# Expert stage of a two-layer kernel: loads, rounding and slot comparison per pair of sequences

## The chip, the core and the metric

The kernel runs on one core of a Trainium2 chip. The metric is device time in microseconds (us); lower is better. The core has TensorE (PE; its weight loads are listed as PEld), VectorE (DVE), ScalarE (ACT), GpSimd (POOL) and SyncE (SP, which here only issues DMAs). Sixteen DMA engines move data between the core's on-chip memory and HBM.

## The reference

128 sequences of 128 tokens with 256 channels pass two layers, each added to its input. The first is windowed cross attention. The second, the stage that is changed here, is a mixture of 16 experts with top-2 routing:

```
xn2  = layernorm(x1)                       # x1: output of the attention layer
p    = softmax(xn2 @ w_router)             # 16 experts
for the 2 best experts e of each token (slots of e filled in token order, 16 slots a sequence; later ones dropped):
    y += p_e * ( silu(s @ w_gate[e]) * (s @ w_fc[e]) ) @ w_proj[e]     # s: the token's row of xn2
out  = x1 + tanh(g_ffn) * y
```

## The kernel before

**Stages.** One program runs three parts one after another: attention (to about 1210 us of the span), routing (softmax, top 2, slot numbers; to about 1264 us), and the expert stage (the rest, about 490 us). Attention leaves `x1_d` (the residual) and `xn2_d` (the normalised rows) in HBM, both laid out as token, sequence, channel. A partition's 256 channels of one sequence are 1 KB there, and those of two neighbouring sequences are 2 KB in one piece.

**Units.** The expert stage works through 128 units, written as a software pipeline over steps u. Each operation has a lag: it serves unit n = u - lag in step u. For loading, picking and dispatching, n is a sequence; eight sequences form a group. For gate, hidden and output, n is a group and a pair of experts, so that eight units cover a group's 16 experts. For fetching and collecting, n is again a sequence. The work of step u, by lag:

- LOAD (-13): SP loads one sequence of `xn2_d` (128 KB) into a ring of three.
- PICK (-11): ACT rounds it to `x_hi` (fp32r); POOL subtracts for the rest, `x_lo`; DVE compares slot numbers with a table for the 0/1 matrix `pick`. Rings of two.
- DISPATCH (-9): PE multiplies `x_hi` and `x_lo` with `pick` into the PSUM bank `DS` (4 matmuls); ACT copies `s_hi`, DVE subtracts for `s_lo`.
- GATE (0): PE forms gate and up projections in `GU` (12 matmuls); ACT takes `th = tanh(gate/2)`; DVE forms `th = (th + 1) * gate` and `hid = th * up`. This is twice silu(gate) * up, and a factor 0.5 in `weight` (line 984) takes the 2 out.
- HIDDEN (2): PE transposes `hid` into `HT`; ACT copies `h_hi`, DVE subtracts for `h_lo`.
- OUTPUT (3): PE forms the down projection `EO` (6 matmuls); ACT copies it to `eo` and issues the store to `eo_d` (256 KB).
- FETCH (12): SP loads one sequence of the residual from `x1_d` into a ring of three; POOL issues two indirect DMAs that gather the token's two expert rows (`first`, `second`) from `eo_d`.
- COLLECT (14): DVE forms `first * weight + residual`, then adds `second * weight`; SP stores the result to `out`.

**Order.** Each engine runs its own list in program order and waits on semaphores. Within a step, PE does OUTPUT, HIDDEN, GATE, DISPATCH. SP does the store of COLLECT, then LOAD, then FETCH. POOL does the two gathers, then `x_lo`. ACT does `eo`, `h_hi`, the store of `eo`, `x_hi`, `th`, `s_hi`. DVE does `h_lo`, `pick`, first half of COLLECT, the two GATE products, second half of COLLECT, `s_lo`.

**Buffers.** `x_in_sb`, `xr` and `y_sb` of this stage are parts of the routing table `scaled`, under whose name their instructions appear in the profile. So `scaled<-xn_d` is LOAD, `scaled<-x_d` the residual's FETCH, `out<-scaled` the store, `scaled<-first,weight,scaled` (L1229) and `scaled<-second,weight,scaled` (L1244) the two halves of COLLECT. `pick<-logits` reads the slot numbers, kept in the old `logits` tensor as fp32.

Of the kernel before, what the change touches and what calls it, by code (L numbers as in the profile page):

```python
# [25 lines left out]
P = 128  # L26
# [833 lines left out]
def routing_block(nc, ctx, T, D):  # L860
# [82 lines left out]
    def _(dve):  # L943
# [40 lines left out]
        then(dve.tensor_scalar(weight[:], prob[:], gates[:, 3:4], 0.5, ALU.mult, ALU.mult))  # L984
# [23 lines left out]
class Unit:  # L1008
# [35 lines left out]
def expert_block(nc, ctx, T, D):  # L1044


    LOAD, PICK, DISPATCH, GATE, HIDDEN, OUTPUT, FETCH, COLLECT = -13, -11, -9, 0, 2, 3, 12, 14
# [8 lines left out]
    def pb(name):  # L1056
# [3 lines left out]
    tiles = T["scaled"][:].rearrange("p b e -> p (b e)").rearrange("p (n c) -> p n c", c=DIM)  # L1060
    x_in_sb, xr, y_sb = tiles[:, 0:3], tiles[:, 3:6], tiles[:, 6:8]
    x_hi = sb("x_hi", [P, 2, DIM], F32R)
    x_lo = sb("x_lo", [P, 2, DIM], F32R)
    pick = sb("pick", [P, 2, SLOTS], F32R)
    s_hi = sb("s_hi", [P, 2, KC, EXPERTS, GROUP, CAP], F32R)
    s_lo = sb("s_lo", [P, 2, KC, EXPERTS, GROUP, CAP], F32R)
    th = sb("th", [P, 2, 2, HID])
    hid = sb("hid", [P, 2, 2, HID])
# [11 lines left out]
    names = ("x_hi_done x_lo_done pick_done ds_done s_hi_done s_lo_done gu_done th_done "  # L1080
             "gated_done hid_done ht_done h_hi_done h_lo_done eo_done eo_copied y_part_done out_done").split()
    M = {n: sem(n) for n in names}
    x_in = [sem(f"xn2_in{r}") for r in range(3)]
# [3 lines left out]
    y_out = [sem("y_out0"), sem("y_out1")]  # L1087
# [28 lines left out]

    def tokens(buf, n):

        return buf[:, n.side, :, :, n.j].rearrange("p k e s -> p (k e) s")

    @block.sync
    def _(sp):
        def step(unit, on):
            n = unit(COLLECT)
            if on(COLLECT):
                sp.wait_ge(M["out_done"], n.n + 1)
                sp.dma_start(D["out"][bass.ds(n.n, 1)].rearrange("b t c -> t b c"),
                             y_sb[:, n.slot(2):n.slot(2) + 1]).then_inc(y_out[n.slot(2)], 16)
# [40 lines left out]
    def _(act):  # L1169
        def step(unit, on):  # L1170
            n = unit(OUTPUT)
            if on(OUTPUT):
                act.wait_ge(M["eo_done"], n.n + 1)
                wait_for(act, eo_out[n.turn(3)], (n - 3).landed(3))
                act.activation(flat(eo[:, n.turn(3)]), EO[n.slot(2)][:], ACT.Copy).then_inc(M["eo_copied"], 1)
# [7 lines left out]
            if on(OUTPUT):  # L1183
                act.wait_ge(M["eo_copied"], n.n + 1)
                act.dma_start(D["eo_d"][n.group][:, n.j * 2:n.j * 2 + 2], eo[:, n.turn(3)]) \
                    .then_inc(eo_out[n.turn(3)], 16)
            n = unit(PICK)
            if on(PICK):
                act.wait_ge(x_in[n.turn(3)], n.landed(3))
                wait_for(act, M["ds_done"], n.n - 1)  # L1190
                act.activation(x_hi[:, n.slot(2)], x_in_sb[:, n.turn(3)], ACT.Copy).then_inc(M["x_hi_done"], 1)  # L1191
            n = unit(GATE)
            if on(GATE):
                act.wait_ge(M["gu_done"], n.n + 1)
# [13 lines left out]
    def _(dve):  # L1208
        def step(unit, on):
            n = unit(HIDDEN)  # L1210
            if on(HIDDEN):
# [3 lines left out]
                                  flat(h_hi[:, n.slot(2)]).bitcast(F32), ALU.subtract).then_inc(M["h_lo_done"], 1)  # L1215
            n = unit(PICK)
            if on(PICK):
                wait_for(dve, M["ds_done"], n.n - 1)
                dve.tensor_tensor(pick[:, n.slot(2)].rearrange("p (e s) -> p e s", s=CAP),
                                  place[:, bass.ds(n.n, 1)].rearrange("p o (e s) -> p (o e) s", s=1)  # L1220
                                  .broadcast_to([P, EXPERTS, CAP]),
                                  iota[:].rearrange("p (e s) -> p e s", s=CAP), ALU.is_equal) \
                    .then_inc(M["pick_done"], 1)
            n = unit(COLLECT)
            if on(COLLECT):
                dve.wait_ge(rows_in[n.turn(3)], n.landed(3, 32))
                dve.wait_ge(x1_in[n.turn(3)], n.landed(3))
                wait_for(dve, y_out[n.slot(2)], (n - 2).landed(2))
                dve.scalar_tensor_tensor(out=y_sb[:, n.slot(2)], in0=first[:, n.turn(3)],  # L1229
                                         scalar=weight[:, 0, bass.ds(n.n, 1)], in1=xr[:, n.turn(3)],  # L1230
                                         op0=ALU.mult, op1=ALU.add).then_inc(M["y_part_done"], 1)
            n = unit(GATE)
            if on(GATE):
                gu = GU[n.slot(2)][:].rearrange("p (e f n) -> p e f n", e=2, f=2)
                dve.wait_ge(M["th_done"], n.n + 1)
                dve.scalar_tensor_tensor(out=th[:, n.slot(2)], in0=th[:, n.slot(2)], scalar=1.0, in1=gu[:, :, 0],  # L1236
                                         op0=ALU.add, op1=ALU.mult).then_inc(M["gated_done"], 1)
                dve.wait_ge(M["gated_done"], n.n + 1)
                wait_for(dve, M["ht_done"], n.n - 1)
                dve.tensor_tensor(hid[:, n.slot(2)], th[:, n.slot(2)], gu[:, :, 1], ALU.mult).then_inc(M["hid_done"], 1)  # L1240
            n = unit(COLLECT)
            if on(COLLECT):
                dve.wait_ge(M["y_part_done"], n.n + 1)
                dve.scalar_tensor_tensor(out=y_sb[:, n.slot(2)], in0=second[:, n.turn(3)],  # L1244
                                         scalar=weight[:, 1, bass.ds(n.n, 1)], in1=y_sb[:, n.slot(2)],
                                         op0=ALU.mult, op1=ALU.add).then_inc(M["out_done"], 1)
# [136 lines left out]
```

## Time and profile before

| | |
|---|---|
| median of 3 timed runs | 1762.0 us (1760.66 to 1764.96) |
| profiled execution, its own time | 1754.3 us |
| its span | 1752.5 us |
| busy PE / DVE / ACT / POOL, whole span | 85% / 80% / 65% / 62% |
| busy PE / DVE / ACT / POOL, 1320 to 1500 us | 88% / 92% / 56% / 82% |
| DMA share 0 to 1146 us; 1320 to 1500 us | 0.23; 0.84 |

The second busy line is worked out from a windows view of the middle of the expert stage. An average over the whole span says little about it, since attention fills two thirds of the span. Matmul records overlap: one of 128x256 is listed with 0.28 us, but the next starts 0.12 us later. A DVE record also runs on a little after the next has begun, so the distance between two starts is what an instruction costs its engine. "issue" as the end of a wait means that the profile shows no releaser.

### The profile page before, as it was taken

How to read it: one execution, taken by the hardware profiler on the slowest of the kernel's cores; microseconds unless marked ns; L12 is line 12 of the kernel's file. 1: busy time of each engine (PE TensorE's matmuls, PEld its weight loads, DVE VectorE, ACT ScalarE, POOL GpSimd, SP SyncE). 2: the span in 40 equal slices, each digit the busy share in tenths (PEclk: the TensorE clock that was granted, in tenths of full speed). 3: DMA queues.
4: the chain of work that ended last, by engine and by line, in shares of the span. 5: the costliest groups of instructions: out<-in, count | busy, mean ns of one | idle time of the engine just before them, and what ended most of it. 6: DMA issues, size and time to landing. Idle time of an engine off the chain costs nothing. (4 is left out here: it accounts for less than half of the span.)

```text
span 1752.5 us, 50746 instructions
## 1 busy us (share of the span) xinstructions
PE 1481.3 (85%) x16844; PEld 1195.2 (68%) x16844; DVE 1408.6 (80%) x2993; ACT 1146.4 (65%) x2321; POOL 1086.1 (62%) x1490
## 2 busy tenths in 40 slices
PE   3899999999999999999999999982199888888881
PEld 3676667777776676777676677761088888888881
DVE  3788888888888888878888888867878999999984
ACT  3777777777777777777777777764065555555550
POOL 3555656565655656565565656534638887888876
PEclk9999999999999999999999999995589999999995
DMA  3122121212222121212212121430037888888887
GB/s 94 50 76 75 61 89 60 90 60 84 65 67 82 60 90 60 90 60 78 71 62 88 60 90 60 137 119 30 15 106 245 260 261 258 261 273 263 264 261 223
DMA packets 156096, 210.21 MB, mean 120 GB/s; under 512 B 18688, under 2 KB 104832, under 8 KB 156032
## 3 DMA queue, kind: packets, MB, share of 16 engines
q1 hardware_dynamic: 125312, 142.36, 25.9%
q0 software_dynamic: 12288, 33.57, 6.7%
q10 hardware_dynamic: 18432, 33.56, 5.3%
q8 instruction: 24, 0.39, 0.1%
q14 instruction: 40, 0.33, 0.1%
HBM read 125.54 MB, written 83.89 MB: 119 GB/s over the span
## 5 line engine op out<-in xcount | busy, mean ns | idle before, releaser
L506 DVE TRANSPOSE_TENSOR_REDUCE part_max<-ST 128x16 f32<-128x512 f32 x512 | 321.3, 685 | 136.6 <-PE ST L685 136.6
L360 ACT ACTIVATE probs_t<-ST 128x512 f32<-128x512 f32 x512 | 264.4, 604 | 27.6 <-PE ST L700 27.4
L712 PE MATMUL PO<-probs_t,v_aug 128*32 128x128 f32 x4096 | 193.6, 284 | 67.9 <-ACT probs_t L360 55.4
L299 POOL TENSOR_TENSOR k_rot<-k_cos,k_sin 128x256 f32<-128x256 f32 x64 | 47.1, 736 | 268.5 <-DVE k_sin L544 268.5
L712 PEld LDWEIGHTS PO<-probs_t,v_aug 128*32 128x32 f32 x4096 | 88.9, 109 | 161.1 <-ACT probs_t L360 154.0
L1191 ACT ACTIVATE x_hi<-scaled 128x256 fp32r<-128x256 f32 x128 | 53.5, 418 | 214.8 <-DMA scaled<-xn_d 168.5
L401 ACT ACTIVATE at_hi<-F 128x512 fp32r<-128x512 f32 x64 | 38.2, 597 | 187.8 <-PE F L730 187.8
L1260 PE MATMUL GU<-we_hi,s_hi 128*128 128x256 f32 x512 | 155.4, 304 | 0.2 <-DVE s_lo L1250 0.2
L1154 POOL DMA_INDIRECT second<-eo_d,collect_row x128 | 123.0, 961 | 42.2 <-issue 28.6
L1163 POOL TENSOR_TENSOR x_lo<-scaled,x_hi 128x256 fp32r<-128x256 f32 x128 | 118.4, 925 | 49.3 <-ACT x_hi L1191 47.3
L1154 POOL DMA_INDIRECT first<-eo_d,collect_row x128 | 124.4, 972 | 37.3 <-issue 20.6
L1261 PE MATMUL GU<-we_hi,s_lo 128*128 128x256 f32 x512 | 144.9, 283 | 0.0
L1262 PE MATMUL GU<-we_lo,s_hi 128*128 128x256 f32 x512 | 144.8, 283 | 0.0
L316 POOL TENSOR_TENSOR q_rest<-q_rot,q_head 128x512 f32<-128x512 f32 x64 | 82.2, 1284 | 78.7 <-ACT q_head L413 78.7
L1260 PE MATMUL EO<-we_hi,h_hi 128*128 128x256 f32 x256 | 81.6, 319 | 50.3 <-issue 43.5
L730 PE MATMUL F<-ident_sb,xn 128*128 128x128 f32 x512 | 86.2, 292 | 31.1 <-ACT xn L437 19.7
L366 ACT ACTIVATE out_t<-PO 128x512 f32<-128x512 f32 x128 | 76.7, 599 | 53.2 <-PE PO L712 53.2
L1229 DVE SCALAR_TENSOR_TENSOR scaled<-first,weight,scaled 128x256 f32<-128x256 f32 x128 | 65.5, 512 | 49.6 <-issue 18.1
L1261 PEld LDWEIGHTS GU<-we_hi,s_lo 128*128 128x128 f32 x512 | 98.3, 192 | 0.0
L1260 PEld LDWEIGHTS GU<-we_hi,s_hi 128*128 128x128 f32 x512 | 97.6, 191 | 0.4 <-issue 0.4
L1262 PEld LDWEIGHTS GU<-we_lo,s_hi 128*128 128x128 f32 x512 | 97.8, 191 | 0.0
L1260 PEld LDWEIGHTS EO<-we_hi,h_hi 128*128 128x128 f32 x256 | 48.3, 188 | 70.0 <-issue 68.1
(158 smaller groups left out, 5610.7 us busy)
## 6 DMA issues: line engine op xcount, KB each, us to landing
eo_d<-eo ACTq DMA_DIRECT2D x128, 256.0 KB
x_in_sb<-x SPq DMA_DIRECT2D x64, 256.0 KB, 2.8
c_in_sb<-ctx_t SPq DMA_DIRECT2D x64, 256.0 KB, 2.9
xr_sb<-x SPq DMA_DIRECT2D x64, 256.0 KB, 4.0
x_d<-x SPq DMA_DIRECT2D x64, 256.0 KB, 4.0
xn_d<-xn SPq DMA_DIRECT2D x64, 256.0 KB, 4.2
scaled<-xn_d SPq DMA_DIRECT2D x128, 128.0 KB, 4.0
scaled<-x_d SPq DMA_DIRECT2D x128, 128.0 KB
```

Of the source, the lines that this page charges most:

```text
L316: pool.tensor_tensor(q_rest[:].rearrange("p k t -> p (k t)"), q_rot[:].rearrange("p k t -> p (k t)"), q_head[:].rearrange("p k t -> p (k t ...
L360: act.activation(probs_t[:, b, i].rearrange("p j q -> p (j q)"), ST[i][:], ACT.Exp) \
L366: act.activation(out_t[:, b].rearrange("p i q -> p (i q)"), PO[:], ACT.Copy).then_inc(M["ot_copied"], 1)
L506: dve.tensor_reduce(part_max[:, i, 0], ST[i][:].rearrange("p (c l) -> p c l", l=32), AX_X, ALU.max, apply_transpose=True).then_inc(M["part ...
L712: last = pe.matmul(PO[32 * j:32 * j + 32, i * SEQ:(i + 1) * SEQ], v_aug[:, n.par, b, head], probs_t[:, b, i, j], start=True, stop=True)
L730: last = pe.transpose(F[:, (2 * k + b) * SEQ:(2 * k + b + 1) * SEQ], src[:, b, k * P:(k + 1) * P], ident[:])
L1154: pool.indirect_dma_start(out=dst[:, n.turn(3)], out_offset=None, in_=D["eo_d"][n.group].rearrange("r e c -> (r e) c"), in_offset=bass.Ind ...
L1163: pool.tensor_tensor(x_lo[:, n.slot(2)], x_in_sb[:, n.turn(3)], x_hi[:, n.slot(2)].bitcast(F32), ALU.subtract).then_inc(M["x_lo_done"], 1)
L1229: dve.scalar_tensor_tensor(out=y_sb[:, n.slot(2)], in0=first[:, n.turn(3)], scalar=weight[:, 0, bass.ds(n.n, 1)], in1=xr[:, n.turn(3)], op ...
L1260: pe.matmul(out, lh, rh, start=first, stop=False)
L1261: pe.matmul(out, ll, rh, start=False, stop=False)
L1262: return pe.matmul(out, lh, rl, start=False, stop=last)
```

## The change

The units, the matmuls and the bytes moved stay as they are. The parts that change:

- SP loads two sequences of `xn2_d` (LOAD, now lag -14) and two of `x1_d` (FETCH, now 13) with one DMA of 256 KB each, in every other step and by turns. SP's order becomes FETCH, LOAD, store.
- The ring of rows holds four sequences, that of residuals six. COLLECT (now 15) works in place in the residual's ring, so that FETCH waits for the stores of the pair six sequences earlier.
- `x_hi` is one ACT instruction per pair (HEAD, -11) on 512 columns. `x_lo` moves from POOL to DVE, one instruction per pair (REST, -10). `pick` is one instruction per pair on DVE, and reads slot numbers kept in bf16. Their rings hold four.
- ACT computes silu directly, so DVE has one GATE product instead of two, and the factor 0.5 is gone.
- ACT does `h_hi` ahead of `eo`. On DVE, `s_lo` stands between the two halves of COLLECT.
- Buffers get fixed places over the routing tables.

```diff
-    LOAD, PICK, DISPATCH, GATE, HIDDEN, OUTPUT, FETCH, COLLECT = -13, -11, -9, 0, 2, 3, 12, 14
+    LOAD, PICK, HEAD, REST, DISPATCH, GATE, HIDDEN, OUTPUT, FETCH, COLLECT = -14, -11, -11, -10, -9, 0, 2, 3, 13, 15
...
+    def two(a, n, ring):
+        return a[:, n.n % ring:n.n % ring + 2]
+    def pair_landed(n, ring):
+        return (n.n // (2 * ring) + 1) * 16
...
     @block.sync
+            n = unit(FETCH)
+            if on(FETCH) and n.n % 2 == 0:
+                if n.n >= 6:
+                    for k in range(2):
+                        sp.wait_ge(y_out[(n.n + k) % 6], n.n // 6 * 16)
+                sp.dma_start(two(xr, n, 6), D["x1_d"][:, bass.ds(n.n, 2)]).then_inc(x1_in[n.n // 2 % 3], 16)
+            n = unit(LOAD)
+            if on(LOAD) and n.n % 2 == 0:
+                wait_for(sp, M["x_hi_done"], n.n // 2 - 1)
+                wait_for(sp, M["x_lo_done"], n.n // 2 - 1)
+                sp.dma_start(two(x_in_sb, n, 4), D["xn2_d"][:, bass.ds(n.n, 2)]).then_inc(x_in[n.n // 2 % 2], 16)
...
-            n = unit(LOAD)
-            if on(LOAD):
-                wait_for(sp, M["x_hi_done"], n.n - 2)
-                wait_for(sp, M["x_lo_done"], n.n - 2)
-                sp.dma_start(x_in_sb[:, n.turn(3):n.turn(3) + 1], D["xn2_d"][:, bass.ds(n.n, 1)]) \
-                    .then_inc(x_in[n.turn(3)], 16)
-            n = unit(FETCH)
-            if on(FETCH):
-                wait_for(sp, M["y_part_done"], n.n - 2)
-                sp.dma_start(xr[:, n.turn(3):n.turn(3) + 1], D["x1_d"][:, bass.ds(n.n, 1)]) \
-                    .then_inc(x1_in[n.turn(3)], 16)
...
     @block.gpsimd
-            n = unit(PICK)
-            if on(PICK):
-                pool.wait_ge(M["x_hi_done"], n.n + 1)
-                wait_for(pool, M["ds_done"], n.n - 1)
-                pool.tensor_tensor(x_lo[:, n.slot(2)], x_in_sb[:, n.turn(3)], x_hi[:, n.slot(2)].bitcast(F32),
-                                   ALU.subtract).then_inc(M["x_lo_done"], 1)
...
     @block.scalar
+            n = unit(HEAD)
+            if on(HEAD) and n.n % 2 == 0:
+                act.wait_ge(x_in[n.n // 2 % 2], pair_landed(n, 2))
+                wait_for(act, M["ds_done"], n.n - 2)
+                act.activation(flat(two(x_hi, n, 4)), flat(two(x_in_sb, n, 4)), ACT.Copy).then_inc(M["x_hi_done"], 1)
...
-                               ACT.Tanh, scale=0.5).then_inc(M["th_done"], 1)
+                               ACT.Silu).then_inc(M["gate_done"], 1)
...
     @block.vector
+            n = unit(REST)
+            if on(REST) and n.n % 2 == 0:
+                dve.wait_ge(M["x_hi_done"], n.n // 2 + 1)
+                wait_for(dve, M["ds_done"], n.n - 2)
+                dve.tensor_tensor(flat(two(x_lo, n, 4)), flat(two(x_in_sb, n, 4)), flat(two(x_hi, n, 4)).bitcast(F32),
+                                  ALU.subtract).then_inc(M["x_lo_done"], 1)
             n = unit(PICK)
+            if on(PICK) and n.n % 2 == 0:
+                wait_for(dve, M["ds_done"], n.n - 2)
+                dve.tensor_tensor(two(pick, n, 4).rearrange("p b (e s) -> p b e s", s=CAP),
...
+                dve.tensor_tensor(gate[:, n.slot(2)], gate[:, n.slot(2)], gu[:, :, 1], ALU.mult).then_inc(M["hid_done"], 1)
...
-                dve.scalar_tensor_tensor(out=th[:, n.slot(2)], in0=th[:, n.slot(2)], scalar=1.0, in1=gu[:, :, 0],
-                                         op0=ALU.add, op1=ALU.mult).then_inc(M["gated_done"], 1)
...
     @block.tensor
-                pe.wait_ge(M["pick_done"], n.n + 1)
-                pe.wait_ge(M["x_hi_done"], n.n + 1)
-                pe.wait_ge(M["x_lo_done"], n.n + 1)
+                for done in ("pick_done", "x_hi_done", "x_lo_done"):
+                    pe.wait_ge(M[done], n.pair + 1)
...
-        T["place"] = T["logits"]
+        T["place"] = sb("place", [P, SEQS, EXPERTS], BF16)
```

DVE in the middle of the stage, one step before (`hid<-th,GU` is the second GATE product):

```order
L1214 TENSOR_TENSOR h_lo<-HT,h_hi 128x256
L1219 TENSOR_TENSOR pick<-logits,iota_sb 128x256
L1229 SCALAR_TENSOR_TENSOR scaled<-first,weight,scaled 128x256
L1236 SCALAR_TENSOR_TENSOR th<-th,GU 128x256
L1240 TENSOR_TENSOR hid<-th,GU 128x256
L1244 SCALAR_TENSOR_TENSOR scaled<-second,weight,scaled 128x256
L1250 TENSOR_TENSOR s_lo<-DS,s_hi 128x32x16
```

The same place now, two steps (`xr` is the residual's ring, `raw` the ring of rows):

```order
L1216 TENSOR_TENSOR h_lo<-HT,h_hi 128x256
L1222 TENSOR_TENSOR x_lo<-raw,x_hi 128x512
L1237 TENSOR_TENSOR gate<-gate,GU 128x256
L1242 SCALAR_TENSOR_TENSOR xr<-first,weight,xr 128x256
L1248 TENSOR_TENSOR s_lo<-DS,s_hi 128x32x16
L1253 SCALAR_TENSOR_TENSOR xr<-second,weight,xr 128x256
L1216 TENSOR_TENSOR h_lo<-HT,h_hi 128x256
L1227 TENSOR_TENSOR pick<-place,iota_sb 128x512
L1237 TENSOR_TENSOR gate<-gate,GU 128x256
L1242 SCALAR_TENSOR_TENSOR xr<-first,weight,xr 128x256
L1248 TENSOR_TENSOR s_lo<-DS,s_hi 128x32x16
L1253 SCALAR_TENSOR_TENSOR xr<-second,weight,xr 128x256
```

Seven instructions a step become six. The second row of a step is by turns the rest or the comparison of a whole pair.

SP in the middle of the stage, two steps before:

```order
L1127 DMA out<-scaled 128x256
L1133 DMA scaled<-xn_d 128x256
L1138 DMA scaled<-x_d 128x256
L1127 DMA out<-scaled 128x256
L1133 DMA scaled<-xn_d 128x256
L1138 DMA scaled<-x_d 128x256
```

And two steps now:

```order
L1142 DMA raw<-xn_d 128x512
L1146 DMA out<-xr 128x256
L1137 DMA xr<-x_d 128x512
L1146 DMA out<-xr 128x256
```

Six DMAs in two steps become four, and each load stands ahead of its step's store.

## Rows read from the trace of the kernel before

**Rows 1.** Windows: length, busy PE PEld DVE ACT POOL, clock, DMA share, GB/s

```profile
1320.00:1500.00 180.00, 157.68 (x1235) 149.04 (x1233) 166.07 (x357) 101.33 (x257) 147.32 (x154) 1.00 0.84 259
```

**Rows 2.** Who waited for whom, 1320 to 1640 us: total us, times, longest

```profile
PE EO L1260 <- issue: 32.4, 78, 1.2
...
DVE scaled L1229 <- DMA second<-eo_d,collect_row: 0.6, 1, 0.6
```

**Rows 3.** Chain that ended last, at 1361 us: start, us, what

```profile
1361.36 0.34 SPq L1127
...
1361.80 0.46 SPq L1133
...
1362.31 3.70 DMA scaled<-x_d
```

**Rows 4.** Timeline of POOL, 1503 to 1507 us: start, us, instruction

```profile
1503.50 0.96 POOL L1154 DMA_INDIRECT first<-eo_d,collect_row  x1 [0.18 <-issue]
1504.77 0.96 POOL L1154 DMA_INDIRECT second<-eo_d,collect_row  x1 [0.30 <-DMA eo_d<-eo]
1505.75 1.01 POOL L1163 TENSOR_TENSOR x_lo<-scaled,x_hi 128x256 fp32r<-128x256 f32 x1
1506.95 0.97 POOL L1154 DMA_INDIRECT first<-eo_d,collect_row  x1 [0.19 <-issue]
```

**Rows 5.** Timeline of DVE, one step in the middle

```profile
1503.57 0.41 DVE L1219 TENSOR_TENSOR pick<-logits,iota_sb 128x256 fp32r<-128x256 f32 x1
1504.42 0.48 DVE L1229 SCALAR_TENSOR_TENSOR scaled<-first,weight,scaled 128x256 f32<-128x256 f32 x1 [0.44 <-issue]
1504.90 0.42 DVE L1236 SCALAR_TENSOR_TENSOR th<-th,GU 128x256 f32<-128x256 f32 x1
1505.35 0.42 DVE L1240 TENSOR_TENSOR hid<-th,GU 128x256 f32<-128x256 f32 x1
1505.69 0.48 DVE L1244 SCALAR_TENSOR_TENSOR scaled<-second,weight,scaled 128x256 f32<-128x256 f32 x1
1506.09 0.68 DVE L1250 TENSOR_TENSOR s_lo<-DS,s_hi 128x512 fp32r<-128x512 f32 x1
1506.69 0.41 DVE L1214 TENSOR_TENSOR h_lo<-HT,h_hi 128x256 fp32r<-128x256 f32 x1
```

**Rows 6.** Windows, a stretch before the first collect

```profile
1300.00:1310.00 10.00, 10.00 (x85) 9.90 (x84) 7.58 (x18) 6.12 (x17) 2.21 (x3) 1.00 0.45 150
```

**Rows 7.** Timeline of DVE: tanh products of units 4, 12, 14, 127

```profile
1295.86 0.42 DVE L1236 SCALAR_TENSOR_TENSOR th<-th,GU 128x256 f32<-128x256 f32 x1 [0.36 <-ACT th L1196]
...
1319.11 0.42 DVE L1236 SCALAR_TENSOR_TENSOR th<-th,GU 128x256 f32<-128x256 f32 x1 [0.35 <-ACT th L1196]
...
1324.91 0.42 DVE L1236 SCALAR_TENSOR_TENSOR th<-th,GU 128x256 f32<-128x256 f32 x1
...
1714.31 0.42 DVE L1236 SCALAR_TENSOR_TENSOR th<-th,GU 128x256 f32<-128x256 f32 x1
```

**Rows 8.** Groups by form, 1320 to 1640 us: busy us, mean ns, idle

```profile
L1244 DVE SCALAR_TENSOR_TENSOR scaled<-second,weight,scaled 128x256 f32<-128x256 f32 x91 | 68.6, 753 | 0.0
...
L1191 ACT ACTIVATE x_hi<-scaled 128x256 fp32r<-128x256 f32 x92 | 38.4, 418 | 133.1 <-DMA scaled<-xn_d 109.3 <-PE DS L1305 23.8
```

**Rows 9.** The subtraction x_lo over the whole span: ns min/median/max

```profile
L1163 POOL TENSOR_TENSOR x_lo<-scaled,x_hi x128: 722/997/1024, 1266.6 to 1682.8; 128x256 fp32r<-128x256 f32 x128
```

**Rows 10.** DMA queues, 1320 to 1640 us: packets, MB, share of 16

```profile
q1 hardware_dynamic: 39074, 35.58, 37.8%
q0 software_dynamic: 8800, 24.02, 25.9%
q10 hardware_dynamic: 13248, 24.12, 20.8%
```

**Rows 11.** Last gather on POOL, and the DVE instruction that waits for it

```profile
1746.11 0.95 POOL L1154 DMA_INDIRECT second<-eo_d,collect_row  x1 [0.31 <-issue]
...
1749.30 0.48 DVE L1229 SCALAR_TENSOR_TENSOR scaled<-first,weight,scaled 128x256 f32<-128x256 f32 x1 [1.43 <-DMA second<-eo_d,collect_row]
```

More of the change, by code:

```diff
@@ L1021, in group, with pair @@
     @property
+    def pair(self):
+        return self.i * (LOOP // 2) + self.c // 2
+    @property
     def group(self):
@@ L1057, in pb @@
         return ctx.enter_context(nc.psum_tensor(name, [P, 512], F32))
[L1060 to L1064, printed above, removed]
+    x_in_sb, xr, x_hi, x_lo = (T[k][:] for k in ("raw", "xr", "x_hi", "x_lo"))
+    pick = sb("pick", [P, 4, SLOTS], F32R)
     s_hi = sb("s_hi", [P, 2, KC, EXPERTS, GROUP, CAP], F32R)
     s_lo = sb("s_lo", [P, 2, KC, EXPERTS, GROUP, CAP], F32R)
-    th = sb("th", [P, 2, 2, HID])
-    hid = sb("hid", [P, 2, 2, HID])
+    gate = sb("gate", [P, 2, 2, HID])
     h_hi = sb("h_hi", [P, 2, 2, P], F32R)
@@ L1086, in expert_block @@
     eo_out = [sem(f"eo_out{r}") for r in range(3)]
-    y_out = [sem("y_out0"), sem("y_out1")]
+    y_out = [sem(f"y_out{r}") for r in range(6)]
     DS = [pb("DS0"), pb("DS1")]
@@ L1170, in step @@
         def step(unit, on):
[L1171 to L1175, printed above, removed]
             n = unit(HIDDEN)
@@ L1183, in step @@
             if on(OUTPUT):
+                act.wait_ge(M["eo_done"], n.n + 1)
+                wait_for(act, eo_out[n.turn(3)], (n - 3).landed(3))
+                act.activation(flat(eo[:, n.turn(3)]), EO[n.slot(2)][:], ACT.Copy).then_inc(M["eo_copied"], 1)
+            n = unit(OUTPUT)
+            if on(OUTPUT):
                 act.wait_ge(M["eo_copied"], n.n + 1)
@@ L1226, in step @@
                 dve.wait_ge(rows_in[n.turn(3)], n.landed(3, 32))
[L1227 to L1230, printed above, removed]
+                dve.wait_ge(x1_in[n.n // 2 % 3], pair_landed(n, 3))
+                dve.scalar_tensor_tensor(out=xr[:, n.turn(6)], in0=first[:, n.turn(3)],
+                                         scalar=weight[:, 0, bass.ds(n.n, 1)], in1=xr[:, n.turn(6)],
                                          op0=ALU.mult, op1=ALU.add).then_inc(M["y_part_done"], 1)
[L1232 to L1235, printed above, removed]
-                dve.scalar_tensor_tensor(out=th[:, n.slot(2)], in0=th[:, n.slot(2)], scalar=1.0, in1=gu[:, :, 0],
-                                         op0=ALU.add, op1=ALU.mult).then_inc(M["gated_done"], 1)
[L1238 to L1246, printed above, removed]
             n = unit(DISPATCH)
@@ L1251, in step @@
                                   tokens(s_hi, n).bitcast(F32), ALU.subtract).then_inc(M["s_lo_done"], 1)
+            n = unit(COLLECT)
+            if on(COLLECT):
+                dve.wait_ge(M["y_part_done"], n.n + 1)
+                dve.scalar_tensor_tensor(out=xr[:, n.turn(6)], in0=second[:, n.turn(3)],
+                                         scalar=weight[:, 1, bass.ds(n.n, 1)], in1=xr[:, n.turn(6)],
+                                         op0=ALU.mult, op1=ALU.add).then_inc(M["out_done"], 1)
         run_flat(dve, step)
@@ L1280, in step @@
                 for e in range(2):
-                    last = pe.transpose(HT[n.slot(2)][:, e * P:(e + 1) * P], hid[:, n.slot(2), e], ident[:])
+                    last = pe.transpose(HT[n.slot(2)][:, e * P:(e + 1) * P], gate[:, n.slot(2), e], ident[:])
                 last.then_inc(M["ht_done"], 1)
```

57 lines of the change are left out of this document (31 added, 26 removed).

## The prediction

> **What bounds the kernel now.** The change touches the expert stage alone, so I read its stretch first, in the windows view [rows 1]. In 180 us of its middle the clock is at 1.00 (2.4 GHz), PE is busy 157.68 us (88%), DVE 166.07 us (92%), POOL 147.32 us (82%), and the DMA engines 0.84. Nothing is at 100%, so the bound is a loop of waits. The length of a step comes from the DVE timeline: unit 14's tanh product starts at 1324.91 and unit 127's at 1714.31 [rows 7], 389.4 us for 113 steps, or 3.446 us each.
>
> The waits say that PE stands before `EO` 78 times in the stretch [rows 2]. `EO` needs `h_lo`, so PE waits for DVE, and DVE waits for something in turn: in the step shown it idles 0.44 us before the first half of COLLECT (L1229) [rows 5]. The chain shows for what [rows 3]. SP issues the store at 1361.36, `xn_d` at 1361.80, then `x_d`, whose data lands 3.70 us after 1362.31, at 1366.01. From the store's issue to the landing is 4.65 us. From L1229's start (1504.42) to the end of L1244 (1505.69 + 0.48) is 1.75 us [rows 5], and a few tenths go to semaphores. The loop is some 6.8 us, and a residual fetched in step u is used in step u+2: 3.4 us a step, as measured.
>
> There is a second bound of the same size. POOL's step [rows 4] is gather 1.27, gather 0.98, `x_lo` 1.20 from start to start, 3.45 us, with gaps of only 0.18 and 0.30 us. Removing one bound alone would gain next to nothing. Here both go.
>
> PE's own pace is in the windows before the first collect: PE 10.00 us of 10.00 [rows 6]. Tanh products of units 4 and 12 start at 1295.86 and 1319.11 [rows 7]: 23.25 / 8 = 2.906 us a step. That is the floor, since the matmuls stay the same.
>
> **The change, part by part (per step).**
>
> *Residual loads.* Fetched one step earlier against COLLECT, ahead of the step's load and store, two at a time. From the end of `out` of n-3, which SP's previous store waits for, to the first half of n there are now three steps less the time from that half's start to the next end of `out`. That time is 0.40 to 0.48 (first half) + 0.60 (`s_lo`) + 0.48 = 1.5 us [rows 5]. SP needs 0.34 + 0.46 us to issue [rows 3] and the data its landing. For 256 KB under load the trace has no row; bounds are 3.70 us (as 128 KB now) and 7.40 us (twice that). The step that this loop needs is (0.8 + 3.7 + 1.5) / 3 = 2.0 us to (0.8 + 7.4 + 1.5) / 3 = 3.23 us. I take it as below the floor, because bytes per step stay equal and 3.70 us contains the queueing behind the `xn_d` load. The stores that free the ring of six are issued over two steps before the fetch, so that wait is covered.
>
> *Row loads.* ACT's idle time before `x_hi`, 109.3 us for `xn_d` [rows 8], is in nobody's way as long as ACT is 56% busy [rows 1]. The new load has three steps less the time that SP waits for `x_lo` of the same step, some 7 us. Price 0. If it came late, ACT would stand with `gate` and `s_hi` queued behind HEAD, and DVE and PE after it.
>
> *POOL.* `x_lo` goes: two gathers are left, 2 x 1.27 = 2.54 us [rows 4]. Below the floor. The gather's loop (two issues 2.5 us, landing 1747.06 to 1749.30 = 2.2 us [rows 11], 1.5 us to the end of `out`) is 6.2 us for three steps, 2.1 us a step. DVE waited for a gather only 0.6 us in the whole stretch, with two steps of distance [rows 2].
>
> *DVE.* I add distances between starts [rows 5]. Before: pick and the like 0.34, first half 0.48, `th` 0.45, `hid` 0.34, second half 0.40, `s_lo` 0.60, `h_lo` 0.34 (same form as `hid`) = 2.95, plus idle, plus what L1244 loses. It has 0.48 us here and 753 ns in the mean [rows 8], so 0.27 more. Now: `h_lo` 0.34, one pair instruction 0.60 (as `s_lo`, also 512 columns; at most twice a `pick`, 0.82), product 0.34, first half 0.40 to 0.48, `s_lo` 0.60, second half 0.40 = 2.7 us; with the upper pair price 2.98. Value 2.72.
>
> L1244 is slow, and POOL's `x_lo` has 722 ns at least but 997 in the median [rows 9]: the two slow each other. The Trainium skill ("SBUF — State Buffer", the section with the single rule on port contention) says that a DVE instruction with two SBUF inputs contends with a GpSimd instruction that reads SBUF, and that the later one is blocked. By that rule the 0.27 us go with `x_lo`, since what stays on POOL are gathers, and DVE needs 2.72 us; if gathers block as well, it needs 2.99 us and sits just above PE. I take the first.
>
> The sum without the page goes by bounds: L1244 between 0.48 and 0.753 us, taken at 0.48, its value in the step shown, where it starts 0.06 us ahead of `x_lo` (1505.69 against 1505.75 [rows 4]). So DVE is at 2.7 us, or at 3.0 us at worst.
>
> *Latencies inside a step.* PE needs `h_lo` a step after the transposes, and DVE's gate product follows PE's gate matmuls with silu between. With DVE at 2.7 of 2.9 us these fit, but with 0.2 us of slack, and single waits will show. I add 0.03 us a step.
>
> *ACT.* One `x_hi` per pair instead of two of 418 ns [rows 8] can only save; silu in place of tanh keeps shape and count. Price 0.
>
> *DMA.* Shares of the three queues [rows 10] sum to 0.845: 0.845 x 3.446 = 2.91 us of all 16 engines per step. Queue 1 moves three transfers of 128 KB a step: 0.378 x 3.446 x 16 / 3 = 6.95 engine-us each. Queue 10 moves one of 256 KB with rows of 2 KB: 0.208 x 3.446 x 16 = 11.5. The two loads' bytes now travel in 2 KB pieces as well: 13.9 becomes 11.5, so 2.91 falls to 2.76 us. Below the floor, but at a share of 0.94.
>
> *Ends.* Ahead of unit 14 nothing of the above binds. The first load is twice as big (up to one landing more, +3.7 us), while the nine dispatches ahead of unit 0 trade POOL's 0.72 us [rows 9] for half of a 0.60 on DVE (-0.4 us each): value 0, bounds -4 and +3.7. At the end COLLECT lies one unit further back, and the tail is paced by POOL's gathers: one pair more, +2.5 us.
>
> **Sum.** 2.906 + 0.03 = 2.94 us a step. 113 x (3.446 - 2.94) = 57.2 us less, 2.5 us more: 54.7 us. The profiled execution has 1754.3 us and would have 1699.6. The timed runs' median, 1762.0, lies 7.7 us above it, and I keep that: 1707 us.
>
> **Rivals.**
>
> *A: DVE or the DMA engines bind between 3.0 and 3.25 us.* For it: the 0.94 share, the landing's upper bound (3.23 us), DVE's upper sum (3.0 us). Against it: DMA work per step falls, and all loops gained a step of distance. At 3.10 us it is 113 x 0.346 = 39 - 2.5 = 36.6 us less: 1725 us. The Trainium skill ("DMA: Bandwidth & Descriptors", table of the Bandwidth section) gives 341 GB/s for transfers of 1 MB and 138 for 64 KB; a step of 2.94 us asks 917,504 B / 2.94 us = 312 GB/s of transfers of 128 and 256 KB. No run here shows that rate over a long stretch; the 259 GB/s at share 0.84 [rows 1] would reach 308 at full share, and 2 KB pieces raise it.
>
> *B: only one of the two bounds went.* If the residual's or the rows' load still limits at 3.3 to 3.44 us, the gain is under 14 us: about 1752. For it: `x_lo` of the same step is waited for by SP, ahead of the store. Against it: that wait ends early in DVE's step.
>
> *C, slower: the paired loads land too late.* Place: SP's one ring, where 256 KB stand in front of each store and each fetch. It decides once a landing takes over 3 x 3.446 - 1.5 - 0.8 = 8.0 us. At 9 us the step is (9 + 2.3) / 3 = 3.77 us, 37 us + 2.5 more: about 1801. For it speaks only the high share; 3.70 us now against it.
>
> **Chances.** Forecast (2.90 to 3.0 us a step, 1700 to 1714) 0.70; A 0.21; B 0.04, a part of it within 0.3% (about 5 us, what a measurement can tell from no change); C 0.04; the rest lies below 1700. The range 1697 to 1733 leaves out B, C and A's upper end. Faster 0.94, within 0.3% 0.02, slower 0.04.
>
> **What would show it.** Steps of 2.9 to 3.0 us between gate products. PE near 10 of 10 us in windows of the middle, and hardly a wait before `EO`. POOL idle about 0.4 us a step before `first`, waiting for the second half of COLLECT. The second half of COLLECT at 0.48 us. The chain through PE lines and no longer through `x_d`. A DMA share of 0.9 or more. I would be wrong with idle time of DVE before the first half of COLLECT for `xr`, with ACT waiting for `raw` and DVE behind it, or with DVE at 98% and PE waiting.

## The result, and the profile after

| | median of the timed runs | runs |
|---|---|---|
| before | 1762.0 us (1758.8 to 1767.1) | 20 |
| after | 1768.2 us (1763.9 to 1771.3) | 20 |

The ratio is 1.0031, with an interval of 1.0021 to 1.0041: slightly slower. Forecast were 1707 us and a range of 1697 to 1733. The profiled execution has 1766.2 us and a span of 1764.4 us, against 1754.3 and 1752.5 before.

The windows view of the changed kernel, the same stretch as [rows 1] (length, busy PE PEld DVE ACT POOL, clock, DMA share, GB/s):

```profile
1320.00:1500.00 180.00, 153.94 (x1224) 148.71 (x1222) 140.33 (x304) 103.75 (x232) 98.49 (x98) 0.98 0.80 256
```

The work left DVE and POOL as forecast (166 to 140 us, 147 to 98 us busy), and yet PE is busy less than before. The granted clock explains little: 0.98 in place of 1.00 costs at most 2% of the stretch, 3.6 us (an estimate), while at the forecast 2.94 us a step it would hold 61 steps and holds 51. The step is in the starts of the gate product, for the same units 14 and 127 as in [rows 7], again a timeline of DVE (start, us, instruction, idle before it and what ended that):

```profile
1325.45 0.42 DVE L1237 TENSOR_TENSOR gate<-gate,GU 128x256 f32<-128x256 f32 x1
...
1724.68 0.42 DVE L1237 TENSOR_TENSOR gate<-gate,GU 128x256 f32<-128x256 f32 x1 [3.99 <-ACT gate L1198]
```

That is 399.2 us for 113 steps, 3.533 us each instead of 3.446, or 9.8 us more; the ends add 2.1 to make the 11.9 us between the spans. Few steps have that length. Some 30 take 2.66 us, and 48 of the 113 over 3.3, up to 5.9. Who waited for whom, 1320 to 1640 us (total us, times, longest), answers to [rows 2]:

```profile
POOL first L1162 <- DVE xr L1253: 78.9, 42, 8.8
...
PE EO L1264 <- ACT h_hi L1177: 29.2, 23, 1.9
ACT s_hi L1204 <- remote: 24.3, 20, 1.7
ACT h_hi L1177 <- remote: 23.2, 24, 1.7
...
ACT gate L1198 <- remote: 13.2, 6, 2.6
```

No load stands in it: neither ACT waits for `raw` nor DVE for `xr`. New is "remote", which the view of before does not contain. All three instructions of ACT wait for PE and for nothing outside this core. The view writes "remote" where the semaphore's update is on record, just before the waiting instruction starts, but over 1.5 us after the end of the last instruction that makes such an update; where the update has no record at all, it writes "issue". One such place, from the timeline:

```profile
1508.44 0.28 PE L1309 MATMUL DS<-pick,x_lo 128*128 128x256 f32 x1
...
1509.32 0.38 PE L1285 MATMUL HT<-ident,gate 128*128 128x128 f32 x2
...
1510.39 0.60 ACT L1204 ACTIVATE s_hi<-DS 128x512 fp32r<-128x512 f32 x1 [1.70 <-remote]
...
1511.90 0.38 ACT L1177 ACTIVATE h_hi<-HT 128x256 fp32r<-128x256 f32 x1 [0.91 <-remote]
...
1512.84 0.36 PE L1264 MATMUL EO<-we_hi,h_hi 128*128 128x256 f32 x1 [1.27 <-ACT h_hi L1177]
```

The last dispatch matmul ends at 1508.72; its semaphore update is recorded at 1510.37, and `s_hi` starts at 1510.39. The transposes start at 1509.32 and end at 1509.69; their update is recorded at 1511.88, 2.2 us later, and `h_hi` starts at 1511.90. ACT was free 0.91 us before that. So ACT reacts at once, and it is the update that comes late. (The ends of matmuls are modelled; in every trace of chips 7 and 13 the update lies within 0.02 us of them.)

From 1320 to 1640 us the trace holds 266 updates made by PE, of which 115 are recorded over 0.8 us after the matmul's end (the transposes' mostly 2.2, the dispatch's 1.6); of the 550 by ACT and DVE not one is even 0.15 us late. The late ones come in PE's order: here dispatch, output, transposes, gate and dispatch again are recorded 1.6, 1.7, 2.2, 0.9 and 0.5 us after their ends. That is what a backlog looks like that fills and drains.

The chain that ended last says the same (start, us, what); its share of "another core or an unknown queue" is 26.6% from 1480 to 1520 us:

```profile
1508.33 2.04 another core or an unknown queue
1510.41 1.46 another core or an unknown queue
1511.90 0.39 ACT h_hi L1177
1512.29 0.55 issue
1512.84 0.36 PE EO L1264
```

So the gain is taken back by PE's updates reaching ACT 1.6 to 2.2 us after the work is done, in about a third of the steps. Whether the paired loads do it was what the experiments had to find. The third and fourth group of them show that they do not, and that it goes with the chip that the kernel runs on, or with what surrounds it there. What delays the updates stays open.

### The profile page after: what moved, and what is told of

The parts are those of the page before. It is cut to its first block and busy times, and to the rows that moved or that the text cites. A ratio compares the mean times of both kernels' runs of the same rounds, so it can differ in the third digit from the quotient of the medians.

```text
span 1764.4 us, 50002 instructions
## 1 busy us (share of the span) xinstructions
PE 1473.3 (84%) x16843; PEld 1196.5 (68%) x16844; DVE 1357.5 (77%) x2865; ACT 1152.6 (65%) x2258; POOL 977.3 (55%) x1362
## 5 line engine op out<-in xcount | busy, mean ns | idle before, releaser
L360 ACT ACTIVATE probs_t<-ST 128x512 f32<-128x512 f32 x512 | 264.4, 604 | 26.6 <-PE ST L700 26.6
L1162 POOL DMA_INDIRECT first<-eo_d,collect_row x128 | 134.3, 1049 | 209.4 <-DVE xr L1253 100.7
L401 ACT ACTIVATE at_hi<-F 128x512 fp32r<-128x512 f32 x64 | 38.2, 597 | 187.0 <-PE F L730 187.0
L1264 PE MATMUL EO<-we_hi,h_hi 128*128 128x256 f32 x256 | 78.9, 308 | 66.0 <-ACT h_hi L1177 38.2
L1248 DVE TENSOR_TENSOR s_lo<-DS,s_hi 128x512 fp32r<-128x512 f32 x128 | 88.0, 688 | 36.9 <-issue 26.0
L1204 ACT ACTIVATE s_hi<-DS 128x512 fp32r<-128x512 f32 x128 | 76.0, 594 | 45.9 <-remote 30.3
L1237 DVE TENSOR_TENSOR gate<-gate,GU 128x256 f32<-128x256 f32 x128 | 53.8, 421 | 67.0 <-issue 40.3
```

Source lines behind the costliest of these rows:

```text
L360: act.activation(probs_t[:, b, i].rearrange("p j q -> p (j q)"), ST[i][:], ACT.Exp) \
L1162: pool.indirect_dma_start(out=dst[:, n.turn(3)], out_offset=None, in_=D["eo_d"][n.group].rearrange("r e c -> (r e) c"), in_offset=bass.Ind ...
L1204: act.activation(tokens(s_hi, n), DS[n.slot(2)][:].rearrange("p (k e s) -> p (k e) s", k=KC, s=CAP), ACT.Copy).then_inc(M["s_hi_done"], 1)
L1248: dve.tensor_tensor(tokens(s_lo, n), DS[n.slot(2)][:].rearrange("p (k e s) -> p (k e) s", k=KC, s=CAP), tokens(s_hi, n).bitcast(F32), ALU. ...
L1264: pe.matmul(out, lh, rh, start=first, stop=False)
```

## The experiments

Five groups; each ran on one chip, with the kernel before beside it. "Step" is (start of unit 127's gate product minus unit 14's) / 113. "Records" counts the recorded semaphore updates, those of DMAs included, per us from 1340 to 1640 us in each trace. "Late" gives, for 1320 to 1640 us, how many of PE's recorded updates come over 0.8 us after the matmul's end. No update of ACT, DVE or POOL is late in any trace.

| run | chip | this, us | before beside it | step, us | records per us | late |
|---|---|---|---|---|---|---|
| e1 single loads | 13 | 1696.8 | 1758.2 | 2.91 | 37 | 0 of 437 |
| e2 tanh | 13 | 1717.6 | 1758.2 | 3.09 | 30 | 0 of 412 |
| e3 x_lo on POOL | 13 | 1763.9 | 1758.2 | 3.51 | 26 | 0 of 359 |
| e4 no residual | 13 | 1692.3 | 1758.2 | 2.85 | 30 | 0 of 441 |
| f1 pair residual | 11 | 1765.1 | 1763.0 | 3.51 | 13 | 114 of 253 |
| f2 pair rows | 11 | 1764.9 | 1763.0 | 3.50 | 13 | 116 of 276 |
| f3 half partitions | 11 | 1778.9 | 1763.0 | 3.63 | 12 | 122 of 259 |
| f4 DVE extra | 11 | 1736.9 | 1763.0 | 3.21 | 12 | 10 of 292 |
| **g1 after, unaltered** | 7 | **1695.7** | 1758.5 | 2.87 | 32 | 0 of 440 |
| g2 single loads | 7 | 1697.2 | 1758.5 | 2.90 | 37 | 0 of 436 |
| g3 tanh | 7 | 1716.6 | 1758.5 | 3.08 | 30 | 0 of 412 |
| h1 before, unaltered | 4 | 1763.8 | 1766.0 | 3.53 | 13 | 1 of 206 |
| **h2 after, unaltered** | 4 | **1768.2** | 1766.0 | 3.52 | 12 | 118 of 269 |
| h3 single loads | 4 | 1773.8 | 1766.0 | 3.60 | 13 | 117 of 249 |
| h4 tanh | 4 | 1742.0 | 1766.0 | 3.28 | 11 | 10 of 290 |
| i1 gathers apart | 13 | 1758.7 | 1760.2 | 3.44 | 27 | 0 of 370 |
| i2 no residual | 13 | 1690.4 | 1760.2 | 2.85 | 30 | 0 of 443 |
| i3 paired store | 13 | 1697.8 | 1760.2 | 2.89 | 29 | 0 of 438 |

The trace of before that the prediction was made from has 32 records per us and no late update, that of after 12 and 115 late ones of 266. One of f2's 8 runs took 6362.5 us; nothing explains it.

### First group: undo one part each

**e1, single loads.** Each pair is loaded with two DMAs of 128 KB, at the same places in the order.

```diff
-                sp.dma_start(two(xr, n, 6), D["x1_d"][:, bass.ds(n.n, 2)]).then_inc(...)
+                for k in range(2):
+                    at = n.n % 6 + k
+                    sp.dma_start(xr[:, at:at + 1], D["x1_d"][:, bass.ds(n.n + k, 1)]).then_inc(...)
```

> The changed kernel, but each pair's load is again two DMAs of one sequence (128 KB, rows of 1 KB) issued one behind the other. In the changed kernel ACT starts s_hi and h_hi 1 to 1.7 us after the matmuls they need are over (waits shown as remote), in two of about every six instructions. Theory P (the paired 256 KB loads are what delays the signals): the remote waits go and the time falls to about 1705 to 1720 us. Theory D (a pace under about 3.2 us a step asks more than the DMA side delivers, whatever the packet size): remote waits stay, the time stays within 10 us of 1768 or rises by up to 15, since 1 KB rows cost more DMA time.

1696.8 us (1693.9 to 1699.6), ratio 0.964 (0.958 to 0.971), no "remote" waits. I read this as: the paired loads bring the late updates on. That reading fell later.

**e2, tanh.** Paired loads stay; tanh and the second product on DVE come back.

```diff
-                               ACT.Silu).then_inc(M["gate_done"], 1)
+                               ACT.Tanh, scale=0.5).then_inc(M["gate_done"], 1)
...
+                dve.scalar_tensor_tensor(out=gate[:, n.slot(2)], in0=gate[:, n.slot(2)], scalar=1.0, in1=gu[:, :, 0],
+                                         op0=ALU.add, op1=ALU.mult).then_inc(M["gated_done"], 1)
```

> The changed kernel, but with tanh on ACT and the second gate product on DVE, as before the change. DVE gets 0.45 us a step more. Theory S (silu, or the shorter DVE list, sets off the late signals): they go, and the step is 3.1 to 3.2 us, the time about 1730. Theories P and D: late signals stay where the loads are paired or the pace is high; the time is 1755 to 1775 us. D alone allows that DVE, now at 3.15 us a step, slows the pace enough for the late signals to vanish.

1717.6 us, ratio 0.976 (0.971 to 0.981). Windows of e2:

```profile
1320.00:1500.00 180.00, 176.25 (x1396) 167.28 (x1395) 176.18 (x401) 119.77 (x262) 106.79 (x112) 1.00 0.90 291
```

DVE at 176 of 180 us sets the step of 3.09 us.

**e3, x_lo on POOL.** The paired subtraction moves from DVE to POOL, behind the gathers.

```diff
+                pool.tensor_tensor(flat(two(x_lo, n, 4)), flat(two(x_in_sb, n, 4)), flat(two(x_hi, n, 4)).bitcast(F32),
+                                  ALU.subtract).then_inc(M["x_lo_done"], 1)
```

> The changed kernel, but x_lo is on POOL, one instruction of 512 columns per pair (about 1.5 to 2 us). POOL then needs 2.54 + 0.8 to 1.0 = 3.3 to 3.5 us a step. Theory P: the remote waits stay, the time is over 1768 us. Theory D: POOL holds the pace above 3.3 us, the remote waits vanish, the time is 1745 to 1765 us. A theory that POOL's idle waiting causes them: they vanish as well.

1763.9 us (1761.4 to 1767.2), ratio 1.0027 (1.001 to 1.0044). From its waits, and from its groups by form (busy us, mean ns, idle):

```profile
PE DS L1308 <- POOL x_lo L1171: 51.4, 43, 3.1
```

```profile
L1253 DVE SCALAR_TENSOR_TENSOR xr<-second,weight,xr 128x256 f32<-128x256 f32 x87 | 78.3, 900 | 0.0
...
L1171 POOL TENSOR_TENSOR x_lo<-raw,x_hi 128x512 fp32r<-128x512 f32 x44 | 56.3, 1281 | 0.8
```

PE waits for `x_lo`, and the second half of COLLECT takes 900 ns, as it had 753 in [rows 8]. With this subtraction on POOL nothing is left of the gain, though the residual is still fetched a step earlier. The reverse, `x_lo` on DVE with the residual fetched as before, was not run; so that the residual's loop was a bound of its own is argued from the trace of before and not shown.

**e4, no residual.** The residual is loaded for the first six sequences alone; later ones add what the ring holds.

```diff
+                else:
+                    sp.dma_start(two(xr, n, 6), D["x1_d"][:, bass.ds(n.n, 2)]).then_inc(x1_in[n.n // 2 % 3], 16)
```

> The changed kernel without the residual's loads from the seventh sequence on (the old content of the ring is added instead): 128 KB a step less, 14% of the bytes, all else equal. Theory D: the DMA share at a given pace falls from 0.94 to 0.81, the remote waits vanish or nearly so, the step is 2.85 to 2.95 us and the time about 1705 us. Theory P, if any paired load is enough: half of them are left, remote waits stay in part, the time is 1735 to 1765 us.

1692.3 us: 4 us below e1, the nearest version on this chip. The residual's traffic costs next to nothing.

### Second group: which paired load

**f1 and f2.** e1's edit for the rows alone (the residual stays paired), and for the residual alone.

> Only the residual comes in pairs of 2 KB pieces; each pair of rows is two DMAs of one sequence. Theory 1 (late signals need both kinds of paired load, since the version without residual loads, with paired rows, had none): no waits put down to a releaser outside the core's records, a step of about 2.9 us, 1695 to 1702 us. Theory 2 (the residual's pair alone does it, for it is the one that was missing in the version without residual loads): those waits return, a step near 3.4 us, 1750 to 1770 us. If each pair costs a share of its own: 1725 to 1740 us.

> Only the rows come in pairs; each pair of residuals is two DMAs of one sequence. Theory 1 (both kinds are needed): 1695 to 1702 us and no waits for an unknown releaser. Theory 2 (it is the residual's pair): the same, 1695 to 1702 us. If any paired load does it while the total traffic is there: 1750 to 1770 us. Half each: 1725 to 1740 us.

1765.1 and 1764.9 us, with 50 and 59 us of "remote" waits on ACT in 320. Either pair would then cost the whole gain. **f3** keeps 2 KB pieces but splits each pair into two DMAs of 64 partitions:

```diff
+                for h in (0, 64):
+                    sp.dma_start(two(xr, n, 6)[h:h + 64], D["x1_d"][h:h + 64, bass.ds(n.n, 2)]) \
```

> Both kinds stay paired in pieces of 2 KB, but each pair is two DMAs of 64 partitions (128 KB each). If the length of the pieces is what holds the signals up, nothing changes: 1755 to 1770 us, with the late s_hi and h_hi. If it is the size of one DMA (or how many packets one DMA puts on each of the 16 engines at once), the late signals go: 1695 to 1705 us.

1778.9 us, 11 more than the changed kernel. **f4** adds a DVE instruction that leaves the values alone:

```diff
+                dve.scalar_tensor_tensor(out=gate[:, n.slot(2)], in0=gate[:, n.slot(2)], scalar=1.0,
+                                         in1=gate[:, n.slot(2)], op0=ALU.mult, op1=ALU.max).then_inc(M["same_done"], 1)
```

> The changed kernel with silu and both kinds of paired loads, and one DVE instruction more per step (the gate's maximum with itself, in place, same values), so that DVE paces the step at about 3.1 us as with the tanh version (which measured 1717.6 us). If the pace decides: no late signals, 1712 to 1725 us, faster than the changed kernel although DVE does more. If it is silu or the missing wait between the products: the late signals stay, 1765 to 1790 us.

1736.9 us, 31 us *faster* than the changed kernel's 1768.2 with more work, yet 19 slower than e2, whose list on DVE is as long. That did not fit paired loads as the cause, and the chip was another than in the first group. No run of either group was the changed kernel itself, so this was the next thing to run.

### Third group: the changed kernel itself

Unaltered, with e1's and e2's versions beside it.

> The changed kernel, unaltered, on the same chip and beside the two versions below. The first four experiments ran on one chip, the second four on another, and no run of either held the changed kernel itself. Theory 1 (the late signals come from the 2 KB pieces of the paired loads): 1764 to 1771 us again, with waits for an unknown releaser, wherever it runs. Theory 2 (they are a trait of some chips, and the first four experiments ran on one without it): on a chip without it 1695 to 1702 us, on a chip with it 1764 to 1771.

> The version with all loads single (both kinds, 1 KB pieces), again. Theory 1: 1694 to 1700 us wherever it runs, although pairing either kind alone costs the whole gain. Theory 2: the same time as the unaltered changed kernel beside it, within 5 us, whichever level that is.

> The version with tanh and both products, again, both kinds of loads paired. Theory 1 (2 KB pieces and a pace below 3.1 us): 1716 to 1719 us wherever it runs. Theory 2: on a chip with the trait it loses part of its gain, as the version with the extra DVE instruction did (1736.9 us): 1730 to 1745 us; on a chip without it 1716 to 1719.

**1695.7 us** (1692.6 to 1699.1), ratio 0.964 (0.960 to 0.968), and 1697.2 for single loads. Theory 1 fell: pairing the loads by itself gives and takes nothing here. Windows and units 14 and 127 of g1:

```profile
1320.00:1500.00 180.00, 179.06 (x1494) 177.45 (x1494) 166.23 (x367) 128.29 (x281) 116.68 (x121) 1.00 0.93 309
```

```profile
1327.40 0.42 DVE L1237 TENSOR_TENSOR gate<-gate,GU 128x256 f32<-128x256 f32 x1 [0.30 <-ACT gate L1198]
...
1651.60 0.42 DVE L1237 TENSOR_TENSOR gate<-gate,GU 128x256 f32<-128x256 f32 x1
```

PE is busy 179 of 180 us; 324.2 / 113 = 2.869 us a step. The same place as above in g1's timeline:

```profile
1501.79 0.38 PE L1285 MATMUL HT<-ident,gate 128*128 128x128 f32 x2
...
1502.21 0.39 ACT L1177 ACTIVATE h_hi<-HT 128x256 fp32r<-128x256 f32 x1 [0.34 <-PE HT L1285]
```

Here `h_hi` starts 0.42 us after the transposes start, not 2.58, and the update is recorded 0.02 us after their end. One of the 113 steps takes over 3.3 us, not 48. One kernel, two times.

### Fourth group: both kernels on one chip

> The kernel before, unaltered, for a trace of it from the same chip as the three below. Theory 2 (a trait of the chip or of the placement): on a chip with the trait its records of semaphore updates in the expert stage are incomplete too, though its time stays at 1755 to 1767 us; on a chip without it they are complete, 31 to 32 a us. Theory 3 (the trait is one of the changed kernel alone): complete on every chip.

> The changed kernel, unaltered, a third time. Theory 2: either 1693 to 1700 us or 1764 to 1771 us, nothing between, and all its runs on one chip at one level.

> All loads single. Theory 2, where pairing has no part in it: the level of the unaltered changed kernel beside it, within 6 us. If single loads escape the trait: 1694 to 1700 us also where the changed kernel has 1764 to 1771.

> Tanh and both products, paired loads. Where the changed kernel is at 1693 to 1700 us: 1716 to 1719 us. Where it is at 1764 to 1771: 1730 to 1745 us, as the version with the extra DVE instruction (1736.9 us), so faster than the changed kernel although each step has one DVE instruction more.

This chip was of the other sort. The changed kernel has 1768.2 us (1765.6 to 1772.7), single loads 1773.8: they escape nothing. Tanh has 1742.0 (1737.2 to 1742.0), ratio 0.986 (0.982 to 0.989). Waits of h2 and, in the second fence, of h4:

```profile
ACT s_hi L1204 <- remote: 29.0, 24, 1.9
...
ACT h_hi L1177 <- remote: 27.0, 28, 3.0
```

```profile
ACT s_hi L1204 <- remote: 0.3, 1, 0.3
ACT gate L1198 <- remote: 0.3, 1, 0.3
...
ACT h_hi L1177 <- remote: 0.2, 1, 0.2
```

In h4 and f4, with a DVE instruction more, 10 of some 290 updates are over 0.8 us late, though most of those for the dispatch and the gate matmuls still come 0.1 to 0.7 us late. This fits their being faster than the changed kernel there, and slower than e2 and g3 on chips of the first sort. Why the longer step spares them most of the delay is not shown.

The kernel before, h1, has incomplete records there as well (13 per us), and a span of 1763.0 us instead of 1752.5. Its windows, and its waits before `x_hi` (109.3 and 23.8 us in [rows 8]):

```profile
1320.00:1500.00 180.00, 156.66 (x1207) 148.56 (x1206) 159.30 (x349) 99.33 (x252) 144.76 (x151) 0.98 0.82 253
```

```profile
ACT x_hi L1191 <- DMA scaled<-xn_d: 72.1, 46, 3.7
...
ACT x_hi L1191 <- PE DS L1305: 50.5, 40, 1.9
```

So Theory 2 holds and Theory 3 fell. On this sort of chip before loses some 8 us (1766.0 against 1758.5), the changed kernel 72. h1 has one late update in 206, so its 8 us have another cause, which stays open; part can be the clock (0.98).

### Fifth group: what brings it on

These edits were meant for a chip of the second sort, but ran on chip 13, of the first, which thus showed the same level in both groups that it ran. They say nothing on the late updates; that stays open.

**i1, gathers apart.**

```diff
+                    if k:
+                        pool.wait_ge(M["hid_done"], min(n.n + FETCH + 2, SEQS))
```

> POOL's second gather of a step waits for the gate product of the next step, so the two gathers start over 1.5 us apart, at the same number and bytes. On a chip that records all updates: 1694 to 1702 us. On one that records 13 a us or fewer: if bursts of gathers bring the late signals, 1700 to 1735 us; if not, 1764 to 1780 us.

1758.7 us (1753.5 to 1762.7): a miss. The chip records its updates, and the whole gain is gone all the same. From its waits:

```profile
DVE xr L1244 <- DMA second<-eo_d,collect_row: 62.8, 82, 2.2
POOL second L1164 <- DVE gate L1239: 61.9, 52, 8.5
```

The held back gather lands after DVE wants it, and DVE's lateness holds the next gather back.

**i2, no residual, again**, e4's edit.

> The residual is loaded for the first six sequences alone, later ones add what lies in the ring: 128 KB and 8 semaphore updates a step less of 896 KB and 80 for DMAs. On a chip that records all updates: 1692 us as before. On one that does not: if traffic or the number of updates brings the late signals, 1700 to 1745 us; if only the pace does, 1764 to 1775 us.

1690.4 us, as in the first group. **i3, paired store.**

```diff
-            if on(COLLECT):
+            if on(COLLECT) and n.n % 2:
...
+                sp.dma_start(D["out"][bass.ds(n.n - 1, 2)].rearrange("b t c -> t b c"),
+                             xr[:, at:at + 2]).then_inc(y_out[n.n // 2 % 3], 16)
```

> The results of two sequences are stored with one DMA of 256 KB, in every other step: 8 semaphore updates a step less at the same bytes. On a chip that records all updates: 1694 to 1702 us. On one that does not: if the number of updates counts, 10 to 40 us under the changed kernel's 1768; if it does not, 1764 to 1775 us.

1697.8 us, no better than g1.

## Why the prediction was wrong

The forecast of what the edits do was right in the main; that the hand-overs between engines would stay as the trace of before shows them was not. On chip 7, of the first sort, the changed kernel takes 1695.7 us, 11 under the forecast and just below its range; on the result's it takes 1768.2. Its sum is compared here with g1 and then with the result.

- *DVE, forecast 2.72 us.* Right. The second half of COLLECT fell to its short value, by groups by form of g1:

```profile
L1253 DVE SCALAR_TENSOR_TENSOR xr<-second,weight,xr 128x256 f32<-128x256 f32 x108 | 51.3, 475 | 0.1
```

  475 ns against 753 in [rows 8], and in the result's trace 477, with the gathers still on POOL: gathers do not slow it. e3, with `x_lo` back on POOL, has 900. The rule of the Trainium skill ("SBUF — State Buffer", the section on port contention) agrees with both.
- *POOL, 2.54 us, idle before `first`.* Below the floor, as forecast. The idle time before `first` is 73.8 us for 109 gathers in g1, 0.68 us a step and not 0.4, and what mostly ends it is the store of `eo`, not the second half of COLLECT.

```profile
POOL first L1162 <- DMA eo_d<-eo: 50.4, 68, 7.0
...
DVE xr L1242 <- DMA second<-eo_d,collect_row: 5.4, 14, 1.2
```

- *Residual and row loads, price 0.* Right: no wait for either, and without the residual 1690 to 1692 us, so it costs about 5 us.
- *DMA, 2.76 us, share 0.94.* Right for g1: 0.93 in the window above, at 309 GB/s. Rival A expected such a share to bind; PE at 179 of 180 us says no. e1, with 128 KB for both loads, reached 309 GB/s and a share of 0.95 from 1330 to 1650 us. The bandwidth table of the Trainium skill ("DMA: Bandwidth & Descriptors"), 138 GB/s at 64 KB and 341 at 1 MB, has no row for these sizes; 309 lies between its two, and no wait here shows a limit at it.
- *PE's floor, 2.906 us.* Slightly too high: g1 needs 2.869 us over the whole middle. At units 4 to 12 of the kernel before [rows 7], the waits view lists no wait of PE, so where the 0.04 us went stays open.
- *Ends, +2.5 us.* Too small, they are 6.6. g1 reaches unit 14 2.5 us later than before and has 42.3 us behind unit 127's product instead of 38.2. Its sum is 113 x (3.446 - 2.869) = 65.2, less 2.5, less 4.1: 58.6 us, the difference of the spans.
- *Latencies inside a step, "I add 0.03 us a step".* This is the step that failed. It took the time from PE's last matmul to ACT's start to be what the trace of before shows, give or take single waits. In the result's trace the term is 3.533 - 2.906 = 0.63 us a step, in place of 0.03: 113 x 0.60 = 68 us, which more than covers the 61 by which the forecast missed. ACT waits 60.7 us of 320 there for updates of PE recorded over 1.5 us late ("remote"), and PE 29.2 us for `h_hi` behind them; g1 has neither. The prediction had even noted the slack that is used up here ("0.2 us of slack").
- *"The timed runs' median lies 7.7 us above it, and I keep that."* This took the distance for an offset. The runs of before went from 1758.8 to 1767.1 us, and the medians of before are 1758 to 1760 on chips 7 and 13 and 1763 to 1766 on chips 4 and 11. The trace of before, with 32 records per us, is of the first sort. In g1 the profiled execution and the median are the same 1695.7 us.

None of the rivals was it, nor did any of the signs show by which the prediction said it would be wrong. B's time (1752) was nearest, by another mechanism; C's paired loads hold nothing up, since the waits view of the result's trace has no instruction of ACT or DVE that waits for one.

What is shown: one and the same program has two levels, 1696 and 1768 us; which one goes with the chip or its surroundings (four chips, one of them in two groups); at the upper level PE's semaphore updates come late, in PE's order, and those of the other engines do not, and the trace lacks more than half of all updates; single loads do not help there and a list of DVE that is one instruction longer does (1742 us). Not shown: what makes the updates late. Missing records and late updates go together in every trace of the changed kernel here, but every timed run lists a span and a clock and so was recorded: whether the recording has a part in it, no run tells. The Trainium skill ("NOTIFIC — the notification-queue block", the section "Overflow: three behaviours, one of which stalls the engine") says that the block which carries such records drops them when a queue is full, or holds up their producer, and that its inner pipeline always pushes back. Missing records beside late updates are what that could look like, and its counter of stalls would tell; no run here read it, so this is a guess. Whether bursts, the number of updates or the traffic set it off was tried on the wrong sort of chip. Nor is it known which chip the result's runs were on.

Of the versions with right results the changed kernel is the fastest on chip 7 (g1, level with g2); on chip 13, where it did not run unaltered, e1 and i3 reach the same time. The one that was seen to beat the kernel before on both sorts is e2's, with paired loads, `x_lo` on DVE and tanh: 1716.6 to 1717.6 us and 1742.0 us, ratios 0.976 and 0.986.

## What to carry to other kernels

Before explaining a missing gain by the edit, run the unaltered changed kernel again on the chip where the experiments run; here two groups of experiments seemed to prove that paired loads were at fault, and one control overturned it. A kernel that is tightened until one engine is busy 99% has next to no slack for late hand-overs, so a version a few per cent slower can be the better one where it must run on any chip. When two engines slow each other, as DVE and POOL did here, moving one operation can relieve both at once: without that move (e3) nothing of the gain was left, while leaving out silu (g3) cost 21 us of 63.

## What the runs showed of the hardware

- PE's semaphore updates are recorded 0.01 to 0.02 us after the end of its matmuls in every trace of chips 7 and 13, and in the result's trace up to 2.2 us after it at the same place of the same program; `h_hi` starts 0.42 (g1) and 2.58 us after the start of its transposes. The granted clocks are 1.00 and 0.98.
- In six traces of the changed kernel and its load variants (the result's, f1 to f3, h2, h3) 114 to 122 of 249 to 276 recorded updates of PE came over 0.8 us late, and none of ACT, DVE or POOL.
- On chips 4 and 11 the traces hold 11 to 13 semaphore updates per us in the expert stage, on chips 7 and 13 26 to 37, for the same kernels. In the attention stage all have about 10.
- DMAs of 128 and 256 KB kept up 309 GB/s at a share of 0.93 to 0.95, with PE busy 179 of 180 us (g1).
- A DVE instruction with two inputs in the core's memory (128x256, fp32) took 475 ns in the mean with only gathers on POOL (g1), 753 ns with a 128x256 subtraction there as well (before), and 900 ns with one of 128x512 (e3).
- Halving the number of stores at the same bytes (i3), or of loads (g1 against g2), changed the time by about 2 us or less.
